# Spare identity products in the fill, queries projected ahead of values, and row stores ahead of small transfers

## The reference

```
x += tanh(g_xattn[0]) * attention(K = V = ctx, Q = layernorm(x))      # 16 heads of 8, softmax over the HEAD axis
x += tanh(g_ffn[0])   * top-2 mixture of 8 experts(layernorm(x))      # silu(x w0) * (x w1), then wo; hidden 256
x += tanh(g_xattn[1]) * bidirectional attention(c = layernorm(x), q = ctx)   # trilinear scores, softmax, 4D -> D projection
x += tanh(g_ffn[1])   * quantised feed-forward(layernorm(x))          # weights to {-1, 0, 1}, activations to 8 bits, inner 512
```

## Time and profile before

| | |
|---|---|
| profiled execution | 401.17 us |
| its span, first to last instruction | 399.4 us |
| PE busy | 314.3 us (79%), 3131 products |
| DVE busy | 313.1 us (78%) |
| POOL busy | 299.9 us (75%) |
| ACT busy | 257.4 us (64%) |
| chain that ended last | PE 38%, POOL 23%, DVE 11%, issue 9%, DMA 7%, ACT 6%, SP's queue 4% |

### The profile page before, as it was taken

The page is one execution under the profiler, slowest core; times in us unless marked ns, Lnnn a source line. Parts: engine busy times, 40 slices in busy tenths (PEclk is TensorE's granted clock), DMA queues, the critical chain, the costliest instruction groups (busy, mean ns, idle before and its releaser), DMA issues.

```text
span 399.4 us, 10020 instructions
## 1 busy us (share of the span) xinstructions
PE 314.3 (79%) x3131; PEld 272.7 (68%) x3134; DVE 313.1 (78%) x913; ACT 257.4 (64%) x726; POOL 299.9 (75%) x459
## 2 busy tenths in 40 slices
PE   1222487887999799978988899888987997997775
PEld 1212367786898579867877799677966796995542
DVE  2569977588849997999789979996889868868434
ACT  4235254535665788669856894777657865974764
POOL 4378989799798998899899989998779793343020
PEclk9999999999799999999999999998999999999695
DMA  4967210310230213120501210202200000010000
GB/s 149 295 183 216 82 36 18 105 32 14 74 117 13 60 41 101 42 61 21 143 6 41 86 60 30 85 4 81 73 28 3 15 13 16 0 29 14 2 13 15
DMA packets 34452, 24.15 MB, mean 60 GB/s; under 512 B 3616, under 2 KB 32096, under 8 KB 34400
## 3 DMA queue, kind: packets, MB, share of 16 engines
q1 hardware_dynamic: 33680, 23.32, 19.6%
q10 hardware_dynamic: 720, 0.20, 0.2%
HBM read 16.16 MB, written 7.34 MB: 59 GB/s over the span
## 4 chain that ended last, share of the span: by engine, by line
PE 38%; POOL 23%; DVE 11%; issue 9%; DMA 7%; ACT 6%; SPq 4%; POOLq 0%; DVEq 0%; ACTq 0%
POOL tree L938 9%; PE ps_d L1441 9%; POOL attn L944 7%; PE ps_z L1187 5%; PE ps_z L1188 4%; PE ps_z L1189 4%; DMA k_rows<-rows_dram 3%; PE ps_a L1195 3%; POOL m_h L875 2%; DMA wf_raw<-in_wd 2%; DVE y L1648 2%; SPq L798 2%; DVE shifted L1583 1%; DMA q_rows<-rows_dram 1%; DVE head_max L1577 1%
## 5 line engine op out<-in xcount | busy, mean ns | idle before, releaser
L1187 PE MATMUL ps_z<-m_xhi,w_hi 128*128 128x256 f32 x240 | 77.3, 322 | 14.2 <-DVE m_h L1624 6.7
L944 POOL TENSOR_TENSOR attn<-attn,head_inv 128x1024 f32<-128x1024 f32 x32 | 75.8, 2374 | 0.5 <-DVE head_inv L1599 0.5
L1441 PE MATMUL ps_d<-wdn,m_h 128*128 128x128 f32 x512 | 70.5, 281 | 5.1 <-DVE m_h L1624 2.1
L1188 PE MATMUL ps_z<-m_xhi,w_lo 128*128 128x256 f32 x240 | 69.2, 288 | 0.0
L1189 PE MATMUL ps_z<-m_xlo,w_hi 128*128 128x256 f32 x240 | 69.1, 288 | 0.0
L1441 PEld LDWEIGHTS ps_d<-wdn,m_h 128*128 128x128 f32 x512 | 62.4, 192 | 8.8 <-issue 4.6
L1616 DVE SCALAR_TENSOR_TENSOR m_u<-m_tanh,ps_z 128x256 f32<-128x256 f32 x120 | 49.0, 411 | 18.2 <-ACT m_tanh L1032 17.3
L1032 ACT ACTIVATE m_tanh<-ps_z 128x256 f32<-128x256 f32 x120 | 46.0, 384 | 26.3 <-PE ps_z L1189 25.9
L1187 PEld LDWEIGHTS ps_z<-m_xhi,w_hi 128*128 128x128 f32 x240 | 47.0, 196 | 20.8 <-DVE m_u L1616 7.0
L875 POOL TENSOR_TENSOR m_h<-m_u,m_z 128x256 f32<-128x256 f32 x56 | 41.2, 736 | 18.4 <-DVE m_u L1616 18.4
L938 POOL TENSOR_TENSOR tree<-tree 128x256 f32<-128x256 f32 (+2 forms) x90 | 46.6, 517 | 7.1
(11 more groups left out here) (309 smaller groups left out, 826.3 us busy)
## 6 DMA issues: line engine op xcount, KB each, us to landing
rows_dram<-qk_parts SPq DMA_DIRECT2D x16, 192.0 KB, 2.1
k_rows<-rows_dram SPq DMA_DIRECT2D x16, 192.0 KB
q_rows<-rows_dram SPq DMA_DIRECT2D x16, 192.0 KB
w_raw<-in_w SPq DMA_DIRECT2D x2, 1024.0 KB, 8.2
rows_dram<-qk_parts SPq DMA_DIRECT2D x16, 128.0 KB, 1.8
x_in<-in_x SPq DMA_DIRECT2D x8, 128.0 KB, 2.5
ct_in<-in_ctx_t SPq DMA_DIRECT2D x8, 128.0 KB, 2.6
rows_dram<-qk_parts SPq DMA_DIRECT2D x16, 64.0 KB, 1.8
```

Source lines behind the costliest of these rows:

```text
L944: pool.tensor_tensor(e, e, head_inv[:, u % 2].unsqueeze(1).to_broadcast([P, HEADS, HALF]), ALU.mult).then_inc(s_attn, 1)
L1187: pe.matmul(dst, hi_w, hi_x, start=start, stop=False)
L1188: pe.matmul(dst, lo_w, hi_x, start=False, stop=False)
L1441: last = pe.matmul(ps_d[:, b * P:(b + 1) * P], m_h[:, m % 4, b * P:(b + 1) * P], wdn[:, m], start=(k == 0), stop=(k == TPE - 1))
```

## The change

1. A new entry `pe.warm_s` with 40 due times, 67 or 68 units of the table apart (300 to 2932), places 40 groups of four products of the bf16 identity with itself (128 columns each) in PE's order. The first waits for the constants. Counted in PE's order: 3 groups ahead of the first key product, 5 ahead of the first transposes, 3 ahead of the first query product, 4 ahead of the value product, 4 ahead of the second pair's key product, 6 ahead of the weights' total, 6 ahead of the first scores, 1 ahead of the second pair's transposes, 4 ahead of the second scores, 4 ahead of the second pair's query product.
2. All due times are new, and with them the order on every engine. In the fill:
   - PE: first query product ahead of the value product; second pair's key product ahead of the weights' total; first scores ahead of the second pair's transposes; the second pair's first scores between the two halves of the first pair's first weighted values (before: behind both); first expert tile ahead of the gate product.
   - SP: key stores 0 and 1, the loads of pair 1, key store 2, then the FFN weights, query stores, both fetches, then the seven small DMAs, then the loads of pair 2, key store 0 of pair 1, then `sp.w_late`. `load_res` and `load_f` of the first pair go behind the stores of pair 1.
   - DVE: query scale and low key weights ahead of the first statistics; the scale of the query bias moves from behind the bias parts to ahead of them; the queries' rest, the second pair's statistics and the first `w_lo` ahead of `w_abs`; all three `w_round` and the first `w_clip` ahead of the first maximum, `w_small` and the second `w_clip` behind the first subtraction.
   - ACT: key weights ahead of ct_hi; part1 of the keys ahead of the tanh of the gains, and this ahead of a_xhi; both query parts ahead of all `w_hi`; `gate_hi` just ahead of the first exponential, behind ct_hi of pair 2 and a_xhi of pair 1.
   - POOL: third query part and the second ct_lo ahead of the first `w_lo`.
3. Behind the fill, steps close to one another change places on all engines; no instruction is added or removed there.

```diff
 WHEN = {
-    "sp.load_a": (12, 1501, 2546, 3638, 7464, 12475, 17304, 20931),
+    "sp.load_a": (12, 1041, 2411, 3435, 7236, 12287, 16962, 20480),
     "sp.store_parts": (
-        (1372, 2340, 5666, 9673, 12892, 17404, 21683, 25406),
-        (1416, 2436, 5877, 9884, 13964, 18240, 21883, 25695),
-        (1461, 3048, 6712, 10374, 14327, 18518, 22342, 26965),
-        (1671, 3218, 6753, 10415, 14367, 18559, 22433, 27006),
-        (1816, 3497, 6989, 10630, 14730, 18610, 22609, 27330),
-        (1891, 3739, 7086, 10786, 14806, 18653, 23156, 27406),
+        (875, 2511, 5401, 9373, 12745, 17162, 21316, 25023),
+        (997, 2755, 5526, 9964, 13806, 17657, 21862, 25844),
+        (1142, 2800, 6253, 10286, 14063, 18317, 21957, 26537),
+        (1335, 3144, 6294, 10327, 14104, 18357, 22058, 26578),
+        (1398, 3256, 6762, 10377, 14464, 18408, 22367, 26999),
+        (1473, 3389, 6857, 10550, 14540, 18452, 22808, 27074),
     ),
     "sp.fetch_rows": (
-        (1960, 3826, 7126, 11165, 15185, 19034, 23535, 27447),
-        (2176, 3979, 7280, 10827, 14847, 18694, 23197, 27600),
+        (1537, 3598, 6898, 10929, 14919, 18492, 23187, 27114),
+        (1896, 3751, 7051, 10591, 14581, 18696, 22849, 27268),
     ),
...
     "pe.kq": (
-        (477, 1835, 5419, 9492, 12622, 17139, 21304, 25292),
-        (1523, 3078, 6020, 10201, 14020, 17967, 21982, 26622),
+        (476, 1516, 5184, 9260, 12555, 16844, 21202, 24910),
+        (1033, 2990, 6151, 9957, 13570, 17606, 21811, 26271),
     ),
...
-    "pe.v": (1319, 5085, 8891, 12379, 16864, 20787, 25115, 28897),
+    "pe.v": (1297, 4857, 9020, 12155, 16628, 20495, 24674, 28982),
...
 ONCE = {
     "sp.w_moe": 358,
     "sp.w_out": 113,
-    "sp.w_fin": 1005,
-    "sp.w_ffn": 853,
-    "sp.w_late": 2804,
+    "sp.w_fin": 2042,
+    "sp.w_ffn": 1183,
+    "sp.w_late": 2555,
-    "dve.w_small": 1914,
-    "dve.w_abs": 1556,
-    "dve.w_scale": 1830,
-    "dve.w_round": (1943, 2066, 2386),
-    "dve.w_clip": (2443, 2595),
+    "dve.w_small": 2712,
+    "dve.w_abs": 1771,
+    "dve.w_scale": 2046,
+    "dve.w_round": (2158, 2197, 2237),
+    "dve.w_clip": (2321, 2743),
...
+    "pe.warm_s": (300, 367, 435, 502, 570, 637, 705, 772, 840, 907, 975, 1042, 1110, 1177, 1245, 1312, 1380, 1447, 1515, 1582, 1650, 1717, 1785, 1852, 1920, 1987, 2055, 2122, 2190, 2257, 2325, 2392, 2460, 2527, 2595, 2662, 2730, 2797, 2865, 2932),
 }
...
             for now in order("pe"):
+                for n in range(len(ONCE["pe.warm_s"])):
+                    if due(now, "pe.warm_s", n):
+                        if n == 0:
+                            pe.wait_ge(c_misc, 8)
+                        for k in range(4):
+                            pe.matmul(ps_f[:, 0:P], ident_bf[:], ident_bf[:], start=True, stop=True)
```

More of the change, by code:

```diff
@@ L64 @@
-    "pool.a_rstd": (467, 2292, 3414, 4828, 11299, 16757, 20361, 24484),
-    "pool.ct_lo": (399, 2108, 2915, 8603, 12228, 13500, 20286, 21743),
+        (1537, 3598, 6898, 10929, 14919, 18492, 23187, 27114),
+        (1896, 3751, 7051, 10591, 14581, 18696, 22849, 27268),
+    ),
+    "sp.load_res": (3300, 4917, 8512, 12207, 16426, 21906, 24550, 28749),
+    "sp.load_f": (3904, 11082, 15072, 18874, 23340, 28361, 31165, 34626),
+    "sp.store": (16506, 20269, 24504, 28315, 32267, 35648, 37875, 39131),
@@ L102 @@
-    "act.a_norm": (619, 2451, 3543, 6806, 12380, 17209, 20836, 24936),
-    "act.ct_hi": (340, 2055, 2534, 8320, 9723, 13339, 17931, 21368),
-    "act.a_xhi": (822, 2871, 5804, 9918, 13310, 17762, 21810, 26364),
+        (7232, 10542, 14910, 18950, 23180, 27449, 31151, 33864),
+        (7313, 10988, 15061, 19173, 23329, 27536, 31377, 34436),
+    ),
+    "act.a_norm": (702, 2155, 3340, 6635, 12192, 16867, 20385, 25336),
+    "act.ct_hi": (340, 1593, 2365, 8174, 9579, 12624, 17450, 21177),
+    "act.a_xhi": (905, 2749, 5616, 9774, 12955, 17421, 21642, 25832),
@@ new lines @@
+    "act.top_exp": (6385, 9696, 14075, 17978, 22046, 26273, 30447, 33678),
+    "act.f_norm": (9361, 13420, 17487, 21498, 25670, 29915, 33278, 36407),
+    "act.f_ct": (9616, 13590, 17741, 21850, 25895, 30110, 33503, 36533),
+    "act.f_exp": (9952, 13895, 18011, 22154, 26199, 30463, 33790, 36789),
+    "act.f_an": (10202, 14091, 18150, 22355, 26409, 30636, 33926, 36922),
+    "act.f_at": (10395, 14452, 18502, 22719, 26811, 30837, 34158, 37043),
+    "act.f_exp_max": (10483, 14575, 18644, 22808, 26987, 30935, 34275, 37103),
@@ L261 @@
[L261 to L265 removed]
+        (15321, 19065, 23925, 27400, 31331, 34506, 37068, 39027),
+        (15881, 20010, 24307, 28025, 31962, 35366, 37700, 39076),
+    ),
@@ L266 @@
+    "dve.a_stats": (486, 1342, 3090, 4048, 9167, 14468, 18817, 23142),
+    "dve.m_stats": (4918, 8336, 12343, 16531, 20407, 24634, 28856, 32751),
+    "dve.f_stats": (9074, 12960, 16993, 21156, 25458, 29505, 33058, 36189),
+    "dve.g_stats": (11311, 15306, 19485, 23595, 27765, 31859, 35151, 37569),
+    "dve.a_xlo": (986, 2943, 5658, 9910, 13098, 17559, 21692, 26083),
     "dve.part_rest": (
-        (917, 2289, 5673, 9651, 13097, 17513, 21678, 25437),
-        (1721, 3345, 6709, 10371, 14216, 18179, 22507, 27113),
+        (855, 2276, 5425, 9398, 12824, 17228, 21465, 25030),
+        (1303, 3155, 6500, 10101, 13947, 17805, 22127, 26720),
@@ L327 @@
-    "dve.weights_sum": (7078, 10632, 14713, 18866, 22932, 27158, 31334, 34472),
[9 rows of a table added]
+    ),
+    "dve.logits": (5843, 9562, 13518, 17545, 21936, 25735, 29964, 33564),
+    "dve.top2": (5936, 9699, 14006, 17614, 21989, 26226, 30372, 33623),
+    "dve.weights": (6695, 10192, 14363, 18412, 22505, 26588, 30768, 33892),
+    "dve.weights_sum": (6850, 10395, 14447, 18562, 22653, 26804, 30962, 33975),
     "dve.y": (
[6 rows of a table removed]
-    ),
-    "dve.f_max": (10146, 14053, 18224, 22398, 26415, 30671, 34087, 37053),
-    "dve.f_ainv": (10324, 14261, 18486, 22599, 26646, 30967, 34288, 37273),
@@ new lines @@
+    "dve.f_max": (9810, 13785, 17935, 22055, 26116, 30308, 33706, 36667),
+    "dve.f_ainv": (10146, 13993, 18119, 22289, 26292, 30558, 33878, 36886),
+    "dve.f_max_max": (10437, 14534, 18577, 22766, 26961, 30890, 34240, 37080),
+    "dve.f_q2c": (10859, 14800, 19046, 23109, 27163, 31158, 34577, 37167),
+    "dve.x3": (11213, 15261, 19439, 23550, 27719, 31774, 35001, 37490),
+    "dve.g_amax": (12124, 15894, 20072, 24153, 28266, 32289, 35459, 37883),
+    "dve.g_clamp": (12195, 15965, 20143, 24224, 28592, 32361, 35491, 37915),
```

177 lines of the change are left out of this document (76 added, 101 removed), and 256 rows, old and new, of the table WHEN.

## The result

The changed kernel is slower: 404.15 us median of 20 runs (401.24 to 407.88) against 400.68 us for the kernel before in 20 runs beside it. The ratio is 1.0065, with a 95% interval of 1.0038 to 1.0093. The forecast was 398.6 us, its range ended at 402.8. The profiled execution of the changed kernel took 406.73 us, 404.9 of it span, against 401.17 and 399.4 before; it lies 2.6 us above its kernel's median, so differences between the two traces are larger than those between the medians. All ratios, the means of the clock and its relation to the time leave out the runs over 1.5% above their kernel's fastest (13 of the 217 of the change and the eighteen experiments).

A forecast was written before the change was run, and what follows sets the result against it. Took the fill as bound by a chain of waits through SP's loads and the query fetch, then POOL, later POOL, PE and DVE in turns. Gains of 1.7 + 0.9 = 2.6 us took 401.17 to 398.6 us; range 395.0 to 402.8.

The forecast's parts named there:

- The fetch: Fill, SP: query rows' fetch can start at 19.5 instead of 21.82 us, 2.3 us earlier (bounds 1.7 and 2.9).
- the spares' price of nothing: Fill, PE: 160 spare products charged nothing further; first transposes' move to about 8.6 us put down to DVE's new order.
- The small transfers: Fill, SP: seven small transfers, now between query fetch and pair 2's loads, take 3.3 to 4.0 us.
- The term for the end of the first attention: End of first attention: 1.7 us earlier, taken between 1.0 and 2.4 from the second maximum on DVE.
- The term for the first expert tile: After first attention: first expert product ahead of the gate gains 0.9 us, between 0 and 1.28.
- What is late next: Fill: small transfers delay pair 2's loads, so ct_hi holds the first exponential, only 2.4 us earlier (2.0 to 2.8).
- rival 1: Whole kernel: PE's clock stays up from the fill on, 2.75 us more gain, 395.8 us; chance 0.10.
- The loop behind: After the fill: neighbouring steps change order on all queues, none added; priced at 0, range -1.5 to +1.5 us.
- The forecast's own sign: Wrong if shifts at 50 us and the end differ by over 1.5 us: the loop's order or clock falls.
- Rival 3: Loop: new order opens PE gaps, two more clock falls than today, +3.4 us (404.6); chance 0.15.
- Rival 2: Fill's gain eaten by late small transfers holding DVE or scores waiting for rows: 400 to 401.2 us; chance 0.22.
- rival 4: Loop: one clock fall fewer or a really better order, -3 us beyond the sum, 395.6 us; chance 0.16.

The follow-up runs named there:

- e1: The changed kernel without its 40 groups of spare products, every other order kept: 403.71 us, 1.0055 against the kernel before.
- e14: e3 without the spare products: 399.27 us, 0.9955 against the kernel before.
- e3: Changed order and spares for steps due in the first 54 us, the loop's order of before after that: 399.67 us, 0.9956 against the kernel before.
- e15: e3 with the seven small transfers behind the loads of pair 2 and their scaling behind the second maximum: 400.39 us, 0.9965 against the kernel before.
- e4: Order of before and no spares for the first 56 us, the changed loop order after that: 405.60 us, 1.0111 against the kernel before.
- e5: Changed order and spares for steps due in the first 140 us, order of before after that: 404.22 us, 1.0124 against the kernel before (six runs).
- e18: e3 with four PE steps of the stretch 80 to 92 us put where the change has them: 399.96 us, 0.9979 against the kernel before.
- e2: The kernel before plus the 40 groups of spare products, every other order as before: 400.60 us, 1.0003 against the kernel before.
- e10: Changed order and spares for steps due in the first 89 us, order of before after that: 401.37 us, 1.0006 against the kernel before.

## Why the prediction was wrong

**The fill's sum held, but not by the steps that were priced.** The third query part came at 14.4 against 15.2. The fetch was issued at 20.60, not 19.5, outside the bounds of 18.9 to 20.1, 1.2 us earlier than before where 2.3 were forecast. The FFN weights landed at 19.6 and not at 18.2. The order of the transfers is not at fault: without the spares (e1, e14) the weights are read from 18.37 and 17.86 on and the fetch is issued at 19.44 and 18.92, as forecast. What was wrong is the spares' price of nothing. The forecast put the later transposes down to DVE's new order; they stood at 8.24 us, within the bounds, but at 7.55 in e1 and 7.48 in e14, so the 0.7 to 0.9 us are the spares'. At the normalisations it is 1.1 us (39.65 in e1, 40.76 in the change) and 1.5 (e14, e3). In the ratios no trace of it is left.

The small transfers took 3.3 us, my lower end. ct_hi was last ahead of the first exponential, as said, at 29.54 against 28.9. The second maximum came at 29.59 against 30 to 31, 2.5 us earlier than before, where the first came 2.8 us earlier, so the small scalings took next to nothing from DVE. The term for the end of the first attention, 1.7 us, measured 1.8 by luck: it was taken as DVE's, from the second maximum, but POOL moved with the exponential (1.74 us earlier; tree 1.76, first normalisation 1.76, last three 1.8), and the fourth inverse was done 1.1 us before POOL wanted it. The term for the first expert tile was 0.9 and measured 1.0 (2.8 - 1.8). e15 shows that the step "What is late next" gave a reason and no price: without it the fetch's rows take its place.

**The clock.** It rose at 10 us and was low at 43 us, as forecast; rival 1 fell. The sentence cited from "TensorE: Matmul & The Clock Gate", that low is the default and activity releases it, agrees with the rise at 10 us, with the spares running from 6.09 us on.

**The step that failed is "The loop behind", priced at 0 with -1.5 to +1.5.** e4 measures it: +1.1%, 4.4 us, three times the upper bound. The forecast said that no step is added, only orders of neighbours change, and took that for no cost. It counted one wait of the old trace as the size of what can come or go, where the new order has several at once. The forecast's own sign of this came: the shift at 50 us (1.8 us earlier) and that at the end (5.5 later) differ by far more than 1.5 us. The sum of the rest fits: e3, which is the forecast's case as it was worked out, measured 0.9956, and the forecast's ratio was 0.9935 (2.6 us of 401), inside e3's interval.

**Rival 3** had the sign and nearly the time (404.6), but its mechanism carried the smaller part. It wanted two more falls of the clock. e4 is slower by 4.4 us with 1.4 us more at 1.2 GHz than before, which is worth 0.3 by the relation above; between e3 and e5 the clock accounts for some 1.9 of 6.7 us by the runs, and in their traces the interval with the longer low stretch (pair 2 to 3) for 2.1 of 3.7. So the order costs without any further fall. That the cost consists of waits between engines is seen for 1.4 us (e18) and is my reading for the rest. Rival 2 did not come: 2.8 us of the fill's gain still stood at 58 us, and DVE was not held in front of the second maximum. The new loop is not better (rival 4).

**What stays open.** By which waits most of the loop's 1.1% comes is not settled. In 56 to 95 us the change loses 2.0 us against e3 (transposes of the expert input at 56.00 and 94.85, in e3 at 56.64 and 93.51), and four PE steps explain 1.4 of them by e18. The 2.1 us that it loses from 95 to 137 us go with a low stretch of 10.2 us against 3.4, and e1, in the same order, does not lose them. For the costs behind 140 us no step is named. The table's costs of the order add up to some 3 us of the 4.4, an estimate from its rows; the last 60 us were too different from trace to trace to add them.

## What to carry to other kernels

Price a fill and the loop behind it apart, and never at 0 where an order of many steps is drawn anew: the cheapest test is the new fill with the old loop (here 0.9956, better than both kernels), and a mix of orders of single queues can be worse than either (1.0225). In an order by hand, look between two products that share an accumulation bank for independent work as long as the reading of the bank (here 1.3 us); if an edit moves that work away, the wait shows although no engine has more to do. And a wait that ends last is worth nothing until it is seen what ends next (e15: ct_hi 1.9 us sooner, the exponential not). Spares that change nothing of the whole time need not be free where they stand: here 1.1 to 1.5 us of the fill.

## What the runs showed of the hardware

- 160 spare products in the fill raised PE to 2.4 GHz from 10 to 17 us and from 24 to 30 us and moved the whole time by nothing that can be measured (e2 1.0003, e14 against e3 0.9955 against 0.9956). Beside them the FFN weights were read 1.3 us later (19.62 against 18.37 in e1; 19.19 against 17.86 in e14 beside e3) and the query fetch behind them was issued 1.2 to 1.3 us later. With them a run spends some 63 us at 1.2 GHz by the records, but kernels without them record nothing of the fill, so the two groups can't be compared.
- A run with one us more at 1.2 GHz is 0.19 us longer, not half a us. The Trainium skill ("TensorE: Matmul & The Clock Gate", Terms) estimates the penalty as the throttled time times one minus the ratio, 0.5 here. Measured over the 204 runs it is less than half of that; that PE waits for others in part of the time (it is busy in 79% of the span before) is my reading of why.
- Single low stretches go with somewhat more: from pair 2 to 3 3.4 us for 10.2, 0.33 each (42.76 in the change, 39.37 in e1, the same order); and e10, whose order is that of before from 89 us on, has one at 184.4 to 191.2 us that the kernel before has not, and across it its lag to before grew from 1.2 to 3.0 us: 1.8 us for 6.8, 0.26 each.
